# One expert's weight split moved from VectorE to GpSimd, one moved ahead, and two more fillers

## What is computed

```python
x = x + xattn(layernorm(x), ctx, ctx, Wq, Wk, Wv, Wo, masks)     # (32, 256, 512), 16 heads of 32
pe = make_pe(256, 32)
scores = einsum('sp,tp->st', pe, sign(tile_sigs))                # 8 experts
idx = argmax(scores, axis=-1)                                    # one expert for each position
y_all = einsum('bsd,tod->bsto', layernorm(x), W) + b
out = x + take_along_axis(y_all, idx, ...)                       # the chosen expert's row
```

## Time and profile before

| | |
|---|---|
| median of 3 runs | 871.42 us (871.19 to 871.42) |
| the profiled execution | 871.33 us |
| its span, first to last instruction | 869.5 us |
| TensorE busy | 843.0 us (97%) |
| VectorE busy | 697.8 us (80%) |
| GpSimd busy | 630.0 us (72%) |
| ScalarE busy | 434.9 us (50%) |
| mean granted TensorE clock | 0.99 of full speed |

### The profile page before, as it was taken

How to read it: one execution, slowest core, us unless ns; L and a number is a source line. 1 busy time by engine, 2 the same in 40 slices (tenths; PEclk the granted TensorE clock), 3 DMA queues, 4 the chain that set the end, 5 groups by cost and what they waited for, 6 DMA issues and landing times. The chain is left out here.

```text
span 869.5 us, 19093 instructions
## 1 busy us (share of the span) xinstructions
PE 843.0 (97%) x6509; PEld 676.7 (78%) x6510; DVE 697.8 (80%) x1021; ACT 434.9 (50%) x762; POOL 630.0 (72%) x826
## 2 busy tenths in 40 slices
PE   8999999999999999999999999999993999999996
PEld 6778887778878888778877888777762788888885
DVE  5988888788888888788888888788778877777774
ACT  5655556565755556555756556555465222222221
POOL 3798778686768668686768668685675677777774
PEclk9999999999999999999999999999996999999998
DMA  9613342524252442524243442522488899999993
GB/s 341 226 43 92 116 136 74 171 74 136 74 157 88 135 135 74 170 77 136 74 154 95 132 133 76 162 83 77 141 270 283 256 282 293 291 281 290 286 293 110
DMA packets 123130, 141.70 MB, mean 163 GB/s; under 512 B 16128, under 2 KB 89376, under 8 KB 120992
## 3 DMA queue, kind: packets, MB, share of 16 engines
q1 hardware_dynamic: 108656, 99.45, 36.5%
q0 software_dynamic: 11360, 35.66, 12.8%
q10 hardware_dynamic: 3024, 5.45, 2.2%
HBM read 90.18 MB, written 51.90 MB: 163 GB/s over the span
## 5 line engine op out<-in xcount | busy, mean ns | idle before, releaser
L1827 PE MATMUL pA<-wf_hl,x_hi 128*128 x560 | 139.2, 391 | 1.8 <-DVE wf_hl L356 1.1
L1827 PEld LDWEIGHTS pA<-wf_hl,x_hi 128*128 128x128 f32 x560 | 105.4, 189 | 24.3 <-issue 2.6
L1111 POOL TENSOR_TENSOR s<-s,row 128x1024 f32<-128x1024 f32 x64 | 121.8, 1903 | 3.1 <-DVE row L1371 3.1
L1768 ACT CAST x_hi<-x2t 128x512 fp32r<-128x512 f32 x70 | 43.5, 621 | 147.1 <-PE pA L1827 136.4
L1519 PE MATMUL pS<-wo_hi,ot_hi 128*128 128x512 f32 x256 | 106.9, 418 | 0.3 <-DVE ot_lo L1375 0.3
L1087 POOL TENSOR_SCALAR y_mom<-y_mom 128x1 f32<-128x1 f32 x64 | 15.9, 248 | 124.9 <-DVE y_mom L1392 123.8
L1519 PE MATMUL pS<-xt_hi,wq_hi 128*128 128x512 f32 x256 | 105.3, 411 | 0.2 <-DVE wq_lo L1412 0.2
L1222 ACT CAST ot_hi<-pA 128x512 fp32r<-128x512 f32 x64 | 37.6, 587 | 128.9 <-PE pA L1622 128.8
L1519 PE MATMUL pS<-wo_lo,ot_hi 128*128 128x512 f32 x256 | 100.9, 394 | 0.0
L1519 PE MATMUL pS<-wo_hi,ot_lo 128*128 128x512 f32 x256 | 100.8, 394 | 0.0
L1519 PE MATMUL pS<-xt_lo,wq_hi 128*128 128x512 f32 x256 | 100.6, 393 | 0.0
(11 more groups left out here) (134 smaller groups left out, 1937.6 us busy)
## 6 DMA issues: line engine op xcount, KB each, us to landing
xq<-x_scratch SPq DMA_DIRECT2D x280, 64.0 KB
xt_raw<-in_x_t SPq DMA_DIRECT2D x16, 1024.0 KB, 6.9
x<-in_x SPq DMA_DIRECT2D x64, 256.0 KB, 3.2
y_scratch<-y_biased SPq DMA_DIRECT2D x64, 256.0 KB, 2.1
x_scratch<-y_normal SPq DMA_DIRECT2D x64, 256.0 KB, 2.9
wf_hl<-in_wf ACTq DMA_DIRECT2D x5, 1024.0 KB, 6.1
ctx_raw<-in_ctx_t SPq DMA_DIRECT2D x32, 128.0 KB, 3.0
wf_hl<-in_wf SPq DMA_DIRECT2D x3, 1024.0 KB, 8.7
```

Of the source, the lines that this page charges most:

```text
L1111: pool.tensor_tensor(p, p, h.row[:, t % h.c, 3, :].unsqueeze(2).broadcast_to([P, H, BK]), ALU.mult)\
L1827: return pe.matmul(pA[:, r % 2, :], rows[:, r % 2, c * P:(c + 1) * P], w, start=first, stop=last)
```

## The change

GpSimd splits expert 5 at the end of its attention stage, between raising `wf_lo_pool` and waiting for the stores, and raises `wf_lo_pool` to 3. VectorE no longer splits 5; the split of 6 raises `wf_lo_dve` in its place. The split of 7 moves ahead of transpose 0, and the split of 3 ahead of transpose 1, behind a wait for GpSimd's split. There are ten fillers. The same split stands in the other branch of the kernel (line 612), which does not run with these inputs.

```diff
@@ full_gpsimd (the other branch)
             expert_low(pool, 1, 0, 1).then_inc(wf_lo_pool, 1)
+            expert_low(pool, 5).then_inc(wf_lo_pool, 1)
@@ experts_vector
             dve.sem_inc(wf_lo_ready, 3)
             expert_low(dve, 4)
-            expert_low(dve, 5).then_inc(wf_lo_dve, 1)
-            expert_low(dve, 6)
+            expert_low(dve, 6).then_inc(wf_lo_dve, 1)
+            expert_low(dve, 7)
             transpose(0)
             low(0)
-            expert_low(dve, 7)
+            dve.wait_ge(wf_lo_pool, 3)
+            expert_low(dve, 3).then_inc(wf_lo_ready, NE - 3)
             transpose(1)
             for j in range(NR):
                 if j + 1 < NR:
                     low(j + 1)
                 if j + 2 < NR:
                     transpose(j + 2)
-                if j == 0:
-                    expert_low(dve, 3).then_inc(wf_lo_ready, NE - 3)
                 finish(j)
@@ experts_tensor, body
                     pe.wait_ge(wf_lo_dve, 3)
-                    keep_clock(pe, 8, pT[:, 0, 0:P], ones[:], ones[:])
+                    keep_clock(pe, 10, pT[:, 0, 0:P], ones[:], ones[:])
```

## The result

The changed kernel took **874.36 us** (median of 8 runs, 873.70 to 876.31), the kernel before beside it 871.54 us (8 runs, 871.11 to 871.92). The ratio is 1.0031, with a 95% interval of 1.0021 to 1.0042: slower by 2.82 us in the medians, where 3 us were forecast. The profiled execution took 873.71 us, with a span of 871.9 us.

A forecast was written before the change was run, and what follows sets the result against it. VectorE's chain sets product 2's start, after which TensorE runs without a wait. 4.27 us of hold by GpSimd's split, less 1.25 at finish 0, plus 0 for fillers, made +3.02 us: 874.4 us, range 872.8 to 875.6.

The forecast's parts named there:

- Whoever is second waits for the other's whole instruction: GpSimd's split meeting VectorE's splits: they exclude each other; GpSimd enters at 661.00, ahead of split 4; chance 0.74.
- not last: Rival at VectorE's splits: GpSimd served last, entering at 667.83; product 2 1.97 us late, 873.4 us; chance 0.08.
- Length of GpSimd's split, 4.54 us: GpSimd's split of expert 5, scaled from a quarter-width subtract: 4.54 us, ending at 665.54.
- the low end of 3.3: Lower bound for GpSimd's split of expert 5, from another GpSimd operation's growth: 3.5 us, lowered to 3.3.
- VectorE 4.27 us late: VectorE's chain from the split of expert 4 on: held by GpSimd's split, 4.27 us late (3.0 to 4.7).
- Gain of 1.25 us by finish 0: Ahead of product 2: one split fewer before finish 0, so product 2 follows product 1 without a gap, 1.25 us gained.
- Ten fillers, nothing: TensorE ahead of product 0: two more fillers net 0.44 us, under the 0.68 us slack before product 1; no cost.
- Gathers, nothing: GpSimd's queue behind its split: first gather near 665.6, landed by about 674.5, before finish 0 at 678.9; no cost.
- Sum +3.02 us: Start of product 2 and the total: 4.27 - 1.25 + 0 = +3.02 us, giving 874.4 us.
- Nothing behind it gives any of it back: TensorE's last piece, 804 matmuls without a wait: any shift of product 2's start moves the end by as much.
- side by side: Rival at 661.0: GpSimd's and VectorE's splits do not hold each other up; 1.25 us gained, 870.2 us; chance 0.13.
- product 1 was said to hang on VectorE: Start of product 1: set by VectorE's transpose 1, so it comes 4.27 us late, at 677.81, whatever the fillers do.

The follow-up runs named there:

- e10: Changed kernel with GpSimd writing zeros to a 3072-column spare tile in place of its split of expert 5: 871.11 us, ratio 0.9985.
- e4: Kernel before with the split of expert 3 moved from ahead of finish 0 to behind finish 1: 870.69 us, ratio 0.9983.
- e2: Changed kernel with eight fillers in place of ten: 874.56 us, ratio 1.0028.
- e8: Kernel before, all splits on VectorE, with split 7 moved ahead of low 0 and split 3 ahead of low 1: 871.19 us, ratio 0.9989.
- e9: Kernel before with GpSimd's last bias ahead of the layer norm's scale, and splits 7 and 3 ahead of low 0 and low 1: 870.71 us, ratio 0.9983.
- e1: Changed kernel without GpSimd's split of expert 5, its semaphore raised at once: 871.37 us, ratio 0.9999.
- e12: Changed kernel with GpSimd's split of expert 5 done in four quarters of 128x512: 874.55 us, ratio 1.0034.
- e5: Changed kernel with VectorE's old order of splits, expert 5 still on GpSimd, and eight fillers: 873.92 us, ratio 1.0021.
- e11: Kernel before with an unused 3400-column spare tile allocated ahead of the expert stage's tiles: 877.61 us, ratio 1.0063.
- e3: Changed kernel with GpSimd writing zeros to a 3400-column spare tile in place of its split of expert 5: 876.03 us, ratio 1.0047.

## Why the prediction was right

The forecast was 874.4 us, 872.8 to 875.6; the median is 874.36 us. The agreement to 0.04 us is luck: the sum was 0.2 us too large, and the kernel before ran at 871.54 us, not at the 871.42 that the sum started from.

- **"Whoever is second waits for the other's whole instruction": right.** GpSimd got in when the split of 2 ended, not beside it and not last. e10 shows the reason: at the same place on GpSimd, an instruction that does not read SBUF holds nothing.
- **Length of GpSimd's split, 4.54 us: 4.37 as read above** (660.60 to 664.97). Scaling the quarter-width row was off by 4%; the low end of 3.3 was much too low.
- **VectorE 4.27 us late: measured 4.08.** From the start of the split of 1 to the end of that of 4 it was 663.42 - 655.63 = 7.79 us before and 667.11 - 655.24 = 11.87 after. The 2.15 us from GpSimd's end to VectorE's came out as 2.14.
- **Gain of 1.25 us by finish 0: right in place and about right in size.** Product 2 follows product 1 by 2.85 us (2.83 expected). Late by 4.09 at product 1, 2.86 at product 2: 1.23 us gained. e4 shows the mechanism by itself (1.26 us from product 1, 1.13 us in all).
- **Ten fillers, nothing: right**, with 0.16 us idle ahead of product 1 where 0.24 were worked out. e2 shows it.
- **Gathers, nothing: right.** The first ran from 665.13 to 668.09, and no engine waited for one.
- **Sum +3.02 us: +2.86 at product 2, +2.79 at the end of the span.**

Two steps were less sure than they read. "Nothing behind it gives any of it back" held in the change, where +2.86 us became +2.79, and for the leads of e8, e9 and e10. It did not hold in the profiled executions of e1 and e4, which lost 1.8 us each inside the stage, nor in e12, whose delay grew by 1.5 us. The rival "side by side" was priced too well: e10, which is that case, gained 0.80 us in the medians and 0.90 at product 2, not 1.25; the missing 0.35 us were lost ahead of product 1, at the cast of block 0. And product 1 was said to hang on VectorE; in the changed kernel product 0 ended as late as that cast, and in e5, with one split fewer in front, product 1 hung on product 0.

## What to carry to other kernels

Idle time of GpSimd beside VectorE is only worth something for work that does not read SBUF while VectorE reads two tiles: here 4.4 us of GpSimd saved 2.3 us of VectorE and held it for 4.1. Before an operation is moved to an idle engine, look in the trace for a pair of such operations that met, and read which of the two rows is long. And where a wait is put down to an instruction, ask which semaphore the waiting one needs: changing the order on VectorE alone (e8) gave as much at product 2 as the change does without its hold.

## What the runs showed of the hardware that was not expected

- **Where tiles lie changes the speed of TensorE.** 13,600 unused bytes in each partition, placed ahead of `x2_hi` and `x2_lo`, made each matmul of 512 columns take 395 to 396 ns, not 389: 5.35 us over 67 products. The kernel was 0.63% slower (interval 0.48 to 0.78%), the late cast in e11 included. 12,288 bytes had no such effect (e10). 13,600 is no multiple of 64, and 12,288 is; whether alignment is the cause, and of which tile, was not tried.
- **An experiment's spare tile is itself a change.** e3 alone would have read as "the memset costs more than the split".
- **The expert stage has little room in its transfers.** Between 720 and 760 us the DMA engines were busy for 0.95 of the time in the kernel before (the column ahead of the last):

```profile
720.00:760.00 40.00, 40.00 (x178) 33.13 (x177) 29.29 (x45) 9.11 (x15) 31.17 (x30) 1.00 0.95 293
```

In some executions time was lost in this stage, beside waits for loads (e1), a finish (e4) or scatters (e12); e8, e9 and e10 reached it early and kept their lead. That full transfers are the cause, and that they spread the runs of e1, is argued, not shown. e8's profiled execution, at 872.24 us, was slow for another reason: its last residual came at 654.36 us, 1.78 us later than before.
